# Perceiver layer on one core: the linear attention's stages at other places of each quad

## The reference, cut to what matters

```python
# x: (4, 256, 256), ctx: (4, 4096, 256), 16 heads of 16, everything float32
x = x + xattn(layernorm(x), ctx, ctx, Wq, bq, Wk, bk, Wv, bv, Wh, bh)   # softmax attention over 4096 rows
x = x + attn(layernorm(x), Wqkv, bqkv, Wout, bout, omega, nodes, weights)
x = x + ffn(layernorm(x), w_gate, w_up, w_down)                         # silu(gate) * up, down

# attn, the linear attention:
q, k, v = split(x @ Wqkv + bqkv)
def features(t):                        # t / |t| per head
    proj = einsum('bhtd,rhdm->rbhtm', t, omega)
    return exp(clip(proj * sqrt(2 s) - s, -20, 20)) * factors      # 64 features per head
qf, kf = features(q), features(k)
out[t] = sum_{u <= t} (qf[t] . kf[u]) v[u] / max(sum_{u <= t} qf[t] . kf[u], 1e-6)
```

## Time and profile before

| what | value |
|---|---|
| median of 3 runs | 1024.28 us (1021.52 to 1024.69) |
| profiled execution: time | 1023.58 us |
| profiled execution: span in the trace | 1021.9 us |
| mean granted clock of TensorE | 0.958 |
| TensorE matmul / weight load, busy | 891.8 us / 619.7 us |
| ScalarE / VectorE / GpSimd, busy | 546.9 us / 497.6 us / 111.9 us |
| quads 10 to 21 of batches 1, 2, 3 (with the linear attention) | 85.30 us each |

### The profile page before, as it was taken

One profiled execution on the slowest core, in us unless ns is written; L12 is line 12 of the kernel. 1 busy time (PEld: TensorE's weight loads), 2 busy tenths in 40 slices (PEclk: granted clock), 3 DMA queues, 4 the chain that ended last, 5 costly groups with the idle time before them and its releaser, 6 DMA issues.

```text
span 1021.9 us, 20838 instructions
## 1 busy us (share of the span) xinstructions
PE 891.8 (87%) x8819; PEld 619.7 (61%) x8819; DVE 497.6 (49%) x831; ACT 546.9 (54%) x597; POOL 111.9 (11%) x132
## 2 busy tenths in 40 slices
PE   5699699977999898898899898989899999977865
PEld 4566466645666666665566665665566666656654
DVE  6523135553544346764544345765454445614546
ACT  6177477755565655646465655646466566820101
POOL 1042000000231100000140100000041000004210
PEclk9799899999999999999899999999899999999798
DMA  6898998796866666377866666386967565120000
GB/s 173 147 198 234 154 150 182 146 165 87 173 125 118 111 115 114 101 116 114 187 111 118 107 121 119 89 135 106 180 105 128 103 114 102 14 42 1 1 1 13
DMA packets 59282, 118.00 MB, mean 115 GB/s; under 512 B 23152, under 2 KB 30320, under 8 KB 55728
## 3 DMA queue, kind: packets, MB, share of 16 engines
q1 hardware_dynamic: 57392, 112.22, 60.1%
q0 software_dynamic: 1792, 4.40, 1.5%
HBM read 78.84 MB, written 37.75 MB: 114 GB/s over the span
## 4 chain that ended last, share of the span: by engine, by line
PE 59%; DVE 12%; DMA 11%; issue 6%; ACT 5%; SPq 3%; DVEq 2%; POOL 2%; POOLq 0%; ACTq 0%
PE ps_o L712 16%; PE ps_s L724 12%; PE ps_p L563 7%; PE ps_p L530 7%; DMA kstack<-kscr 7%; ACT probs L993 4%; PE ps_a L656 3%; DVE kfeat L1238 2%; SPq L376 2%; PE ps_a L682 2%; PE ps_a L650 2%; DMA kscr<-kparts 2%; DMA qstack<-qscr 2%; PE ps_a L669 2%; PE ps_a L593 1%
## 5 line engine op out<-in xcount | busy, mean ns | idle before, releaser
L993 ACT ACTIVATE probs<-ps_s 128x1024 f32<-128x1024 f32 x512 | 495.6, 1024 | 289.6 <-PE ps_s L724 266.7
L712 PE MATMUL ps_o<-probs,values 128*17 128x256 f32 x4096 | 258.5, 388 | 0.0
L724 PE MATMUL ps_s<-qstack,kstack 64*128 64x256 f32 x2048 | 206.3, 315 | 56.5 <-DMA kstack<-kscr 34.0
L724 PEld LDWEIGHTS ps_s<-qstack,kstack 64*128 64x128 f32 x2048 | 145.0, 191 | 160.9 <-ACT probs L993 66.5
L712 PEld LDWEIGHTS ps_o<-probs,values 128*17 128x17 f32 x4096 | 106.9, 98 | 95.6 <-issue 12.1
L1030 DVE TENSOR_SCALAR kparts<-ps_p,b_heads 128x512 fp32r<-128x512 f32 x64 | 48.0, 750 | 101.8 <-PE ps_p L530 101.7
L563 PE MATMUL ps_p<-wv_hi,ctx_hi 128*128 128x256 f32 x256 | 79.5, 310 | 1.7 <-DVE wv_lo L1018 1.6
L968 ACT ACTIVATE feat<-feat,node_neg 128x512 f32<-128x512 f32 x32 | 23.1, 722 | 106.9 <-DVE feat L1222 106.9
L1047 DVE TENSOR_TENSOR values<-ps_p,bv_pair 128x512 f32<-128x512 f32 x64 | 44.1, 690 | 66.2 <-PE ps_p L563 66.0
L563 PE MATMUL ps_p<-wv_hi,ctx_lo 128*128 128x256 f32 x256 | 73.0, 285 | 0.0
L563 PE MATMUL ps_p<-wv_lo,ctx_hi 128*128 128x256 f32 x256 | 73.0, 285 | 0.0
(11 more groups left out here) (213 smaller groups left out, 1030.5 us busy)
## 6 DMA issues: line engine op xcount, KB each, us to landing
kstack<-kscr SPq DMA_DIRECT2D x192, 256.0 KB, 9.5
kscr<-kparts SPq DMA_DIRECT2D x64, 512.0 KB, 3.1
ctx_raw<-ctxT SPq DMA_DIRECT2D x32, 512.0 KB, 13.5
qstack<-qscr SPq DMA_DIRECT2D x24, 128.0 KB, 5.2
qscr<-qparts SPq DMA_DIRECT2D x4, 512.0 KB, 3.9
xh<-x SPq DMA_DIRECT2D x4, 256.0 KB, 12.5
xs<-x SPq DMA_DIRECT2D x4, 256.0 KB, 3.7
oscr<-y SPq DMA_DIRECT2D x8, 128.0 KB, 3.6
```

What stands on the lines that cost most here:

```text
L712: last = mm(ps_o[32 * j:32 * j + DH + 1, g * S:(g + 1) * S], values[par][:, i, head_of_step(g, j), :], prob[:, j * S:(j + 1) * S], start=b ...
L724: last = mm(ps_s[s % 2][:, j * S:(j + 1) * S], kstack[par][rows, u, i * P:(i + 1) * P], queries[rows, u, :], start=True, stop=True)
L993: nc.scalar.activation(probs[n % AHEAD][:, :], ps_s[n % 2][:, :], ACT.Exp, scale=float(DH) ** -0.5).then_inc(fast["exp_done"], 1)
```

## The change

The rule that gives the linear attention's stages their steps is another. In the first quad of a pass they go to slots 0 and 1 instead of 2 and 3; in the second and third quad to the third and fourth place of the quad instead of the first and second; in the last quad of a pass to slots 12, 14 and 15 instead of 12, 13 and 14. The stages' order, their number and all instructions stay, and so does every other stage.

```diff
 LINEAR_AT = [QUAD * quad + place for quad in range(10, 22)
-             for place in ((2, 3) if quad % QUAD == 0 else (0, 1, 2) if quad % QUAD == 3 else (0, 1))]
+             for place in ((0, 1) if quad % QUAD == 0 else (0, 2, 3) if quad % QUAD == 3 else (2, 3))]
```

## The result

| | before | after |
|---|---|---|
| median of the runs | 1023.55 us (4) | 1048.99 us (1045.91 to 1051.61, 4) |
| profiled span | 1021.9 us | 1046.9 us |
| quads 10 to 21, batches 1, 2, 3 | 85.30, 85.30, 85.30 | 92.82, 92.53, 92.32 |

The changed kernel takes 1.025 times as long as the kernel before (95% interval 1.0216 to 1.0283), 25.4 us more. The forecast was 1044 us, slower by 20.

A forecast was written before the change was run, and what follows sets the result against it. It took TensorE's order of work and waits as the bound (matmuls cover 87% of the span). Quads 10 to 21 go from 85.30 to 91.96 us, 20.0 us over three batches, giving 1044 us; range 1033 to 1054, about 0.85.

The forecast's parts named there:

- The bank between X and Y: Adjacent tail stages X, Y share ps_a; Y waits for VectorE's emptying, 0.90 us after an A, 1.26 after a feat.
- the 5.4 us that the prediction estimated by that rule: Y's first weight load on TensorE taken ahead of its wait: 36 x 0.15 = 5.4 us less, 1038 us.
- The sum by quads: Quads 10 to 21 priced by TensorE pieces: 91.96 us against 85.30, 6.7 us more in each of three batches.
- What lies outside: Passes outside the moved stages' quads, and the last batch's tail: nothing; a pass changing by over a us counts against it.
- The gains inside the sum: In the twelve quads, late exps and score waits go; without the new waits a batch would be 6.1 us shorter.
- Rival 1: Wait between X and Y below 0.51 us a pair, so faster; at no wait 18 us less, 1006 us; chance 0.04.
- Rival 2: Y waits only for the emptying, 0.56 and 0.81 us: +6, 1030 us; chance 0.04, and 0.03 within 3 us.
- Rival 3: ScalarE becomes the bound as delayed value steps hold the fourth exp: 14 us at 1 us later, 1058; chance 0.05.
- Rival 4: Longer TensorE idle brings the 1.2 GHz clock: 15 us at 10 us a batch, 1059 us; chance 0.04.
- Rival 5: The 27 places don't move as said, and A1, A6, pv2 keeping their slots make it void: 1024 us; chance 0.01.

The follow-up runs named there:

- adjacent, in the old half: Kernel before, stages in their old halves, but both stages of a pair directly behind each other ahead of the unit: 1044.5 us, ratio 1.0167.
- a second bank in the new half: Changed kernel with its places, but the second stage of nine of the twelve pairs goes to bank ps_p: 1020.34 us, ratio 0.9954.
- the stages in two halves: Kernel before with one stage of each pair in the first half, the other in the second, last quads of passes unchanged: 1017.33 us, ratio 0.9934.
- the kernel with values first: Changed kernel, value products ahead of the stages in second halves of quads 10 to 21, except first quads of passes: 1061.73 us, ratio 1.0369.

## Why the prediction was right, point by point

**The bank between X and Y: right, and shown.** The waits appear in the profile after, twelve a batch, named as forecast. They come without the new half (adjacent, in the old half), go with a second bank in the new half, and grow with the emptying only where nothing covers it. Start of X to start of Y in quad 13 is 329.65 - 327.61 = 2.04 us, as in the sum; by the starts, Y comes 2.03 or 2.04 us after a feat (five times a batch) and 1.57 us after an A (seven times), for 2.04 and 1.58 in the sum. The twelve waits add up to 12.4 us of idle weight loads; the sum had 12.8. The weight load was not taken ahead of the wait: load and matmul of A4 both start at 329.65, the load after 1.31 us of idle time, and in all 36 waits of the profile the two start together. The Trainium skill (TensorE: Matmul & The Clock Gate, "Architectural detail: the array is 16× 32×32, not 1× 128×128") says that TensorE's queue can pull a weight load ahead of matmuls in flight. The trace of after does not show it for a load behind the wait, so the 5.4 us that the prediction estimated by that rule did not come.

**The sum by quads** (both halves together, batch 3; first the forecast, then the trace):

| quad | 10 | 11 | 12 | 13 | 14 | 15 | 16 | 17 | 18 | 19 | 20 | 21 |
|---|---|---|---|---|---|---|---|---|---|---|---|---|
| forecast | 8.37 | 8.37 | 7.20 | 7.69 | 7.28 | 7.79 | 7.83 | 7.23 | 7.28 | 8.49 | 7.37 | 7.06 |
| after | 8.36 | 8.32 | 7.19 | 7.71 | 7.45 | 7.69 | 7.82 | 7.46 | 7.40 | 8.49 | 7.35 | 7.08 |

Ten of twelve are within 0.12 us. The two others hold the one price for which no row stood: a feat before value products. I took 0.85; it is 338.59 - 337.53 = 1.06 us:

```profile
337.53 1.13 PE L650 MATMUL ps_a<-qkT,om_sb 128*128 128x256 f32 x4 [0.65 <-DVE amat L1226]
...
338.59 1.92 PE L712 MATMUL ps_o<-probs,values 128*17 128x256 f32 x32
```

That is 0.2 us in two quads of three batches, 1.3 us. In batches 1 and 2 quad 14's first half took 2.95 and 2.62 us instead of 2.27; in batch 1 a matmul of the scores there stands behind 0.41 us of idle time for which the profile names no cause. It is 1.0 us in all, and its cause is open. The three stretches came to 21.8 us, not 20.0; the other quads together were some 0.5 us shorter than the sum.

**What lies outside** is 3.2 us in the profile (2.1 before the first score, 3.1 in passes outside the twelve quads, 2.0 less behind the last). I had put it at nothing, and had written that passes outside the stretches that change by more than a us would make the prediction wrong. By that sign it was wrong on this point: the passes from quad 22 of batch 1 to the start of batch 2 took 77.57 us before and 78.63 after. The granted clock differed there. The same passes in three kernels, the kernel before, the changed one and the one with the stages in two halves:

```profile
382.68:460.25 77.57, 69.79 (x689) 49.11 (x686) 52.78 (x87) 42.65 (x52) 1.39 (x2) 0.98 0.60 111
393.60:472.23 78.63, 70.85 (x689) 49.86 (x686) 52.82 (x87) 42.66 (x52) 1.40 (x2) 0.96 0.58 106
380.96:457.04 76.08, 68.32 (x690) 48.24 (x686) 52.71 (x87) 42.68 (x52) 1.40 (x2) 1.00 0.62 115
```

The same work took 76.08, 77.57 and 78.63 us at a mean granted clock of 1.00, 0.98 and 0.96. The changed kernel run again took 77.61 us at 0.98 there and had its 0.96 in batch 2, so this differs between executions of one program. Over the whole span the clock was 0.953 in the first profile after and 0.958 before, which makes some 98 us against 86 at the 1.2 GHz level, an estimate from these means. That can hold the 3.2 us, but how they divide is not shown, and the medians of the first comparison, 25.4 us apart, can't tell them from the change.

**The gains inside the sum: right.** Quad 15 became shorter, 7.7 us for 8.34, since the late exp of a feature and the wait behind the keys went; ScalarE's wait for features fell from 12.6 to 0.2 us in the stretch, and the scores' matmuls, which waited for exps seven times (3.0 us), did so once (0.4 us).

**Rival 1 (faster)** names what did decide: at waits below half a us a pair the change would have won. The second bank shows that side: 1020 us, with three waits still there. **Rival 2** (only the emptying counts) is refuted by the 2.04 us from X to Y. **Rival 3** (ScalarE): it did wait, 2.5 us in nine second halves a batch, and had slack, as the sum said; the kernel with values first has hardly any such wait and no second half of it is shorter. **Rival 4** (clock): it held at 1.00 in all stretches of the changed kernel. With values first it fell once in each stretch, at quad 20. Batch 1 there (windows view of that kernel):

```profile
382.00:387.00 5.00, 3.01 (x18) 2.38 (x19) 3.34 (x5) 2.66 (x3) 1.19 (x2) 1.00 1.11 154
387.00:392.00 5.00, 5.00 (x39) 3.59 (x37) 0.56 (x1) 1.94 (x2) 0.00 (x0) 0.66 0.91 108
```

Matmuls were busy for 3.0 of 5 us, with one wait of 1.84, and in the next 5 us the mean granted clock was 0.66, so two thirds of them were at the 1.2 GHz level. Quad 20's halves took 5.7 and 4.4 us, for 4.1 and 3.3 in the changed kernel; 1.2 of these 2.7 us are the longer wait before A14 (2.76 us from start to start instead of 1.57), and some 1.5 are left for the clock. A long wait alone doesn't bring it down: pv0 in quad 12 waited 1.85 us, and from 317 to 322 us matmuls were busy for only 2.5 of 5, with the clock at 1.00 there and behind it. What decides between the two is not shown.

```profile
317.00:322.00 5.00, 2.49 (x16) 1.89 (x16) 3.91 (x5) 2.66 (x3) 1.19 (x2) 1.00 0.81 122
```

**Rival 5** (the change doesn't do what it says) did not come: the stages stand at their new places in the timeline.

## What to carry to other kernels

When products share one PSUM bank, look at what stands between two of them on TensorE: the emptying of the first must fit under it, together with all that is queued ahead of the emptying on its engine. A place with nothing beside it is worth nothing in itself; here a projection unit beside the stages was not a load on them but their cover. Price an order by its pieces from start to start in the timeline, a half at a time; the order that leaves no pair uncovered was then found on paper before it ran.

## What the hardware showed that I had not expected

Two copies in a row on VectorE out of one bank start 0.47 us apart though each is shown with 0.56 us. A feature's product takes 0.78 us from its start to the next ahead of a key or value unit (feat1 in the kernel before), 0.96 ahead of scores (feat4 there) and 1.06 ahead of value products (feat4 in the changed kernel). And the clock, which held through twelve waits of 0.7 to 0.9 us between matmuls in each stretch of the changed kernel, fell once a batch with the values first, behind a wait of 1.84 us, though it had held behind one of 1.85. Outside the stretches its mean differed between executions of one program, and the same passes took 76.1 to 78.8 us with it.
